# Masked pooling of blocks 3 to 7: transposes and products replaced by running maxima and scans

## The chip, the cores and the metric

The kernel runs on one core of a Trainium2 chip. The metric is device time in microseconds (us) from start to end of one execution. TensorE (PE) does the matrix products, VectorE (DVE), ScalarE (ACT) and GpSimd (POOL) the rest, and SyncE's queue (SP) issues most of the loads. Each engine runs its own instruction list in order; they meet at semaphores.

## The reference

The input is 16 sequences of 256 tokens with 256 features. Four layers follow each other, each added to its input. Layer 0 makes 16 exponential moving averages of a gated input, mixes them and normalises. Layer 1 is the pooling that changes here. Layers 2 and 3 are a mixture of experts and a head, and hold nearly all the products.

```python
attn_in = tanh(hidden @ W1 + b1)
scores  = attn_in @ v                          # one score per token
mask    = where(pt == 0, l <= j, where(pt == 1, l >= j, l != j))
p       = softmax(where(mask, scores[l], -1e30), axis=l)
cnt     = sum(mask, axis=l)
pooled  = einsum('bjl,bld->bjd', p, hidden) / cnt
```

The type `pt` belongs to a sequence. Token j averages over the tokens up to itself (type 0), from itself on (type 1), or over all but itself (type 2). The weight of a token l depends on j only through which tokens are allowed and through the maximum that is subtracted.

## The kernel before

Features lie on the 128 partitions (two halves, h), tokens along the free dimension. A block `b` is two sequences, so 512 tokens; there are 8 blocks. The two sequences of a block are its lanes `s` = 0 and 1, and layers 0 and 1 of one lane of one block (a *unit* below) are cut into 47 pieces `j` = 0 to 46.

**Experts.** The rest of the work is 640 steps. A step takes one block and one chunk of 128 hidden features of one of 9 experts (8 and a shared one) or of the head. Every product there is exact to fp32 by three products of rounded parts (`exact_sum`, L601): each operand is a high part plus a low part. A step of an expert is 18 matmuls of 512 columns: `front(i)` does 6 for the gate and 6 for the up projection, `back(i-3)` does 6 for the down projection of the step three earlier. Per step ACT applies Silu (L1128) and rounds the hidden values (L1159), DVE multiplies gate and up (L1474), and POOL makes the low part (L1620). A new chunk of weights is rounded on ACT (L1089) and its low part taken on DVE (L1439). `front(i)` on PE waits for the DVE product of step i-2. Where a block ends an expert, DVE adds `ps_out` to the sum in `acc` (L1497), and PE's next `back` waits for that.

**Order.** `order()` (L111) writes one list for all engines. After each step it may emit pieces of the units that are due: each piece has a price in `side_cost` (L92), and a step gives a credit of `pace * step_budget`. A lane gets a second piece in the same step only if that piece has no work on PE. `pace` is set so that a block's units are done before the block joins the experts. Semaphores count stages by name (`SIDE_PE`, `SIDE_ACT`, `SIDE_DVE`, `SIDE_POOL`, L279 to L292).

**Pooling before**, pieces 37 to 46 of a unit. PE makes the attention projection (L797) and the score (L626, one column of weights broadcast, so that every partition holds the score row). The mask is a 128 x 512 table of 0 and -1e30 fetched by an indirect DMA that POOL issues at piece 24 (L1597). DVE adds score and mask (L1244), takes the maximum (L1248) and negates it; ACT takes the exponential with its sum (L942). PE transposes the residual (`xT`, L631), ACT and DVE split it in high and low (L946, L1254); DVE scales the probabilities (L1257, L1259, L1262); PE transposes them (L640), they are split too (L949, L1424), and PE multiplies with twelve matmuls of 256 columns (L805). DVE adds the residual (L1431), which ends the unit ("res").

## Time and profile before

| | |
|---|---|
| three runs | 2800.72, 2802.97, 2803.34 us; median 2802.97 |
| profiled execution | 2801.3 us; its span 2799.5 us |
| granted TensorE clock over the span | 0.999 of full |
| busy, share of the span | PE 99%, DVE 64%, ACT 52%, POOL 44% |
| matmuls | 12802 |

An engine's busy time is the time in which it had at least one instruction running. Matmuls overlap: one of 512 columns is shown as 0.39 us long, while the next starts 0.227 us after it. So for PE the distance between starts tells the cost, not the length. "Idle before" is the time in which an engine had nothing running before an instruction, put down to what released it. Shapes are partitions x elements. The names are those of the program, without buffer numbers.

### The profile page before, as it was taken

The page shows a single profiled execution, that of the slowest core. Times are in us where ns is not written, and L with a number is a line of the kernel's source. Part 1 is how long each engine was busy: PE and PEld are TensorE (multiplying, and loading weights), DVE is VectorE, ACT ScalarE, POOL GpSimd, SP SyncE. Part 2 cuts the span into 40 slices and gives each one's busy share as a digit, 9 for nine tenths or more (in the row PEclk, how much of TensorE's full clock was granted, in tenths as well). Part 3 has the DMA queues.
Part 4 walks back from the last instruction along what each step waited for, and adds up shares of the span by engine and source line. Part 5 has one row for each costly group of instructions (what it writes and reads, how often), then busy time and mean ns, then how long its engine had stood idle before and what let it go on. Part 6 is the DMA issues. An engine that isn't in the chain of part 4 may idle for free.

```text
span 2799.5 us, 36722 instructions
## 1 busy us (share of the span) xinstructions
PE 2767.4 (99%) x12802; PEld 2297.9 (82%) x12802; DVE 1798.8 (64%) x2977; ACT 1452.8 (52%) x2634; POOL 1218.7 (44%) x953
## 2 busy tenths in 40 slices
PE   8899999999999999999999999999999999999999
PEld 5678888888878888888888888888888888888888
DVE  8799778867777666557755766555766563333443
ACT  4655656565447544555545644444644563333445
POOL 6266335533554355424543345433454333333334
PEclk9999999999999999999999999999999999999999
DMA  4344333433223322122321332212322131111222
GB/s 152 103 138 126 93 113 110 134 95 108 76 65 107 95 68 68 55 60 72 100 66 58 85 91 74 63 53 57 108 80 64 43 101 46 46 45 46 79 89 58
DMA packets 117383, 230.37 MB, mean 82 GB/s; under 512 B 13672, under 2 KB 58960, under 8 KB 117200
## 3 DMA queue, kind: packets, MB, share of 16 engines
q1 hardware_dynamic: 81808, 190.15, 22.3%
q10 hardware_dynamic: 32832, 29.49, 4.4%
q0 software_dynamic: 2560, 8.39, 1.0%
q8 instruction: 102, 1.67, 0.2%
q14 instruction: 81, 0.66, 0.1%
HBM read 219.89 MB, written 8.09 MB: 81 GB/s over the span
## 4 chain that ended last, share of the span: by engine, by line
PE 95%; DVE 3%; ACT 1%; issue 1%; DMA 0%; POOL 0%; SPq 0%; DVEq 0%; ACTq 0%
PE bank L605 20%; PE bank L606 20%; PE bank L607 20%; PE ps_out L605 10%; PE ps_out L607 10%; PE ps_out L606 10%; PE bank L598 1%; PE ps_out L598 1%; DVE w_lo L1439 1%; DVE trace L1231 0%; DVE hid L1474 0%; DVE trace L1388 0%; PE bank L824 0%; DMA acc<-in_sidew 0%; PE bank L640 0%
## 5 line engine op out<-in xcount | busy, mean ns | idle before, releaser
L1620 POOL TENSOR_TENSOR hid_lo<-hid,hid_hi 128x512 fp32r<-128x512 f32 x640 | 850.2, 1329 | 1527.8 <-ACT hid_hi L1159 1527.5
L605 PE MATMUL bank<-res_lo,w_hi 128*128 128x512 f32 x2428 | 956.2, 394 | 4.7 <-DVE hid L1474 3.8
L606 PE MATMUL bank<-res_hi,w_lo 128*128 128x512 f32 x2428 | 947.3, 390 | 0.0
L607 PE MATMUL bank<-res_hi,w_hi 128*128 128x512 f32 x2428 | 946.3, 390 | 0.0
L1474 DVE TENSOR_TENSOR hid<-hid,bank 128x512 f32<-128x512 f32 x576 | 394.3, 685 | 618.4 <-PE bank L607 590.9
L1128 ACT ACTIVATE hid<-bank 128x512 f32<-128x512 f32 x576 | 343.9, 597 | 587.6 <-PE bank L607 584.7
L1439 DVE TENSOR_TENSOR w_lo<-w_raw,w_hi 128x768 fp32r<-128x768 f32 (+2 forms) x520 | 497.4, 958 | 191.0 <-ACT w_hi L1089 149.0
L1089 ACT ACTIVATE w_hi<-w_raw 128x768 fp32r<-128x768 f32 x392 | 331.3, 845 | 480.6 <-PE ps_out L607 468.6
L605 PEld LDWEIGHTS bank<-res_lo,w_hi 128*128 128x128 f32 x2428 | 456.4, 188 | 97.0 <-DVE w_lo L1439 4.3
L607 PEld LDWEIGHTS bank<-res_hi,w_hi 128*128 128x128 f32 x2428 | 456.1, 188 | 96.6
L606 PEld LDWEIGHTS bank<-res_hi,w_lo 128*128 128x128 f32 x2428 | 456.5, 188 | 89.4
L605 PE MATMUL ps_out<-hid_lo,w_hi 128*128 128x512 f32 (+1 forms) x1344 | 510.1, 380 | 4.5 <-DVE acc L1497 4.5
L607 PE MATMUL ps_out<-hid_hi,w_hi 128*128 128x512 f32 (+1 forms) x1344 | 510.3, 380 | 0.0
L606 PE MATMUL ps_out<-hid_hi,w_lo 128*128 128x512 f32 (+1 forms) x1344 | 509.9, 379 | 0.0
L1159 ACT ACTIVATE hid_hi<-hid 128x512 fp32r<-128x512 f32 x640 | 399.4, 624 | 13.6 <-DVE hid L1474 12.9
L1607 POOL TENSOR_TENSOR temporal<-temporal,trace 128x512 f32<-128x512 f32 x239 | 326.9, 1368 | 22.4 <-DVE trace L1231 22.1
L1231 DVE TENSOR_TENSOR_SCAN trace<-bank,trace 128x256 f32<-128x256 f32 x480 | 304.8, 677 | 8.2
L605 PEld LDWEIGHTS ps_out<-hid_lo,w_hi 128*128 128x128 f32 x1344 | 252.6, 188 | 56.2 <-issue 5.7
L606 PEld LDWEIGHTS ps_out<-hid_hi,w_lo 128*128 128x128 f32 x1344 | 252.7, 188 | 49.4
L607 PEld LDWEIGHTS ps_out<-hid_hi,w_hi 128*128 128x128 f32 x1344 | 252.6, 188 | 47.4
L1388 DVE SCALAR_TENSOR_TENSOR trace<-gated,bl,bank 128x256 f32<-128x256 f32 x448 | 193.4, 473 | 2.0 <-ACT bank L1080 2.0
L1497 DVE SCALAR_TENSOR_TENSOR acc<-ps_out,coef,acc 128x256 f32<-128x256 f32 x288 | 119.4, 476 | 1.9 <-PE ps_out L607 1.5
(223 smaller groups left out, 1604.5 us busy)
## 6 DMA issues: line engine op xcount, KB each, us to landing
w_raw<-in_chunks SPq DMA_DIRECT2D x392, 384.0 KB, 3.1
mod_on<-mod_rows ACTq DMA_DIRECT2D x154, 128.0 KB, 3.2
w_raw<-in_head_chunks SPq DMA_DIRECT2D x64, 224.0 KB, 2.5
stat<-mod_rows ACTq DMA_DIRECT2D x70, 128.0 KB, 3.2
x_in<-in_xT SPq DMA_DIRECT2D x16, 256.0 KB, 3.6
pre_x<-in_xT SPq DMA_DIRECT2D x14, 256.0 KB, 7.1
soma_rows<-pre_soma SPq DMA_DIRECT2D x14, 256.0 KB, 2.0
soma<-soma_rows SPq DMA_DIRECT2D x14, 256.0 KB, 3.7
```

The costliest lines, as they stand in the source:

```text
L605: mm(out, wh, xl, start=start and i == 0, stop=False, skip_group_check=not lone)
L606: mm(out, wl, xh, start=False, stop=False, skip_group_check=not lone)
L607: last = mm(out, wh, xh, start=False, stop=end, skip_group_check=not lone)
L1089: last = activate(w_hi[k][:], raw[:], ACT.Copy)
L1128: activate(h[:], ps_gate[i % 2][:], ACT.Silu).then_inc(s_act, 1)
L1159: activate(hid_hi[i % DEPTH][:], hid[i % 3][:], ACT.Copy).then_inc(s_hhi, 1)
L1231: return V.tensor_tensor_scan(out, decay.broadcast_to([P, S]), x, 0.0, ALU.mult, ALU.add)
L1388: last = STT(tr[:, h, :], gated[s][:, h, :], bl[:, h, d:d + 1], ps[:, 0:S], ALU.mult, ALU.mult)
L1439: return TT(w_lo[k][:, cols], src, f(w_hi[k][:, cols]), ALU.subtract)
L1474: TT(h[:], h[:], ps_up[i % 2][:], ALU.mult).then_inc(s_hid, 1)
L1607: nc.gpsimd.tensor_tensor(temporal[s][:], temporal[s][:], trace[s][d % 3][:], ALU.add).then_inc(l_pool[s], 1)
L1620: nc.gpsimd.tensor_tensor(hid_lo[i % DEPTH][:], hid[i % 3][:], f(hid_hi[i % DEPTH][:]), ALU.subtract).then_inc(s_hlo, 1)
```

## The change

Blocks 0 to 2 keep the pooling above. For blocks 3 to 7 (ten units) `scanned(b)` is true, and pieces 37 to 46 do other work. The score row s is scanned forwards and backwards for a running maximum (`tops`). With m the running maximum, the weighted sum of the tokens up to j obeys sum(j) = exp(m(j-1) - m(j)) * sum(j-1) + exp(s(j) - m(j)) * x(j): a scan with a decay, and the same backwards. Forward sum, own token and backward sum are each weighted by a share, and a share is zero (its exponent -1e30) where the type does not allow that part. The score matrix of 128 x 512, the fetched mask, both transposes, their splits and the twelve matmuls are gone in these units.

```diff
+SCAN_FROM = 3
+def scanned(b):
+    return b >= SCAN_FROM
@@ side_cost
+    if scanned(b) and j > 36:
+        return (0.7, 1.6, 2.3, 1.5, 2.0, 1.4, 1.9, 2.5, 0.4, 2.5)[j - 37]
@@ order
-                    if lane in touched and (j in ON_PE or j == 25):
+                    if lane in touched and (j in ON_PE or j == 25 or scanned(x) and j > 36):
@@ PE: attention projection at 37, score at 38, then nothing more
-                elif j == 38:
+                elif j == (37 if scanned(b) else 38):
+                elif scanned(b):
+                    if j == 38:
+                        score_and_turns(b, s, j)
@@ ACT
+                    elif j == 40:
+                        act.wait_ge(l_dve[s], dve_at(s, b, "grown"))
+                        activate(trace[s][1][:], trace[s][1][:], ACT.Exp).then_inc(l_act[s], 1)
+                        act.wait_ge(l_pool[s], pool_at(s, b, "decay"))
+                        activate(trace[s][2][:], trace[s][2][:], ACT.Exp).then_inc(l_act[s], 1)
+                    elif j == 41:
+                        act.wait_ge(l_dve[s], dve_at(s, b, "shares"))
+                        activate(shares[s][:, 0, 1:S], shares[s][:, 0, 1:S], ACT.Exp)
+                        activate(shares[s][:, 1, 0:S - 1], shares[s][:, 1, 0:S - 1], ACT.Exp)
+                        activate(owns[s][:, 0, :], owns[s][:, 0, :], ACT.Exp).then_inc(l_act[s], 1)
@@ DVE: new pool_by_scans(b, s, j)
+                if j == 38:
+                    V.tensor_tensor_scan(tops[:, 0, :], ones, score, NEG, ALU.mult, ALU.max)
+                    back_scan(tops[:, 1, :], ones, score, NEG, ALU.mult, ALU.max).then_inc(l_dve[s], 1)
+                elif j == 39:
+                    TS(peak, score, no_own, None, ALU.add)
+                    TT(grown[:], score.unsqueeze(1).broadcast_to([P, 2, S]), tops[:], ALU.subtract)
+                    STT(peak[:, later], tops[:, 0, past], no_past, peak[:, later], ALU.add, ALU.max)
+                    STT(peak[:, past], tops[:, 1, later], no_next, peak[:, past], ALU.add, ALU.max)
+                elif j == 40:
+                    STT(shares[s][:, 0, later], ...); STT(shares[s][:, 1, past], ...); STT(own, ...)
+                elif j == 41:
+                    dve.wait_ge(l_act[s], act_at(s, b, "decay"))
+                    V.tensor_tensor_scan(ends[:, 0, :], decay[:, 0, :], grown[:, 0, :], 0.0, ALU.mult, ALU.add)
+                    back_scan(ends[:, 1, :], ...); V.tensor_tensor_scan(steps, ...)
+                elif j == 42:
+                    dve.wait_ge(l_pool[s], pool_at(s, b, "before"))
+                    for h in range(DH):
+                        last = V.tensor_tensor_scan(gated[s][:, h, :], decay[:, 0, :], gated[s][:, h, :], ...)
+                elif j == 43:
+                    dve.wait_ge(l_pool[s], pool_at(s, b, "after"))
+                    ... two backward scans; wait for POOL's "den"; STT(den, steps, more, den, ALU.add, ALU.mult)
+                elif j == 44:
+                    V.reciprocal(den, den); TT(shares 0 * den); TT(shares 1 * den)
+                elif j == 46:
+                    dve.wait_ge(l_pool[s], pool_at(s, b, "parts"))
+                    ... STT(out, own, 1.0, x1) x2; TT(out += gated); TT(out += ema).then_inc  ("res")
@@ POOL: new weigh(b, s, j); the indirect DMA of piece 24 is not issued
+                if j == 39:
+                    ... two MEMSETs of one column; TT(decay 0); TT(decay 1)
+                elif j == 41:
+                    for out, way, name in ((gated[s], 0, "before"), (ema[s], 1, "after")):
+                        TT(out[:], temporal[s][:], grown[:, way, :].unsqueeze(1).broadcast_to([P, DH, S]), ALU.mult)
+                elif j == 42:
+                    G.tensor_copy(den[:, 0:1], own[:, 0:1]); TT(ends 0); TT(ends 1); TT(den); TT(den)
+                elif j == 45:
+                    TT(own, own, den, ALU.mult); TT(gated * share); TT(ema * share)
@@ setup on POOL: 7 operations on 16 columns (kinds, typ); on DVE one MEMSET (unit)
```

Some lines are drawn together here. The new tiles `shares`, `owns` and `dens` lie where `one_hi`, `one_lo` and `two_hi` lie, `ends` is `soma`, and the next block's first pieces wait for "res" of a scanned block instead of "pooled".

What moves on the engines is shown at block 4, lane 0. First DVE, where that unit ends; before (L1431 ends the unit, L1231 is the first scan of the next block):

```order
L1474 TENSOR_TENSOR hid<-hid,bank 128x512 [waits up,activated]
L1424 TENSOR_TENSOR two_lo<-bank,two_hi 128x512 [waits lane0_act]
L1403 TENSOR_TENSOR two_lo<-trace_0,two_hi 128x512 [waits lane1_act]
L1474 TENSOR_TENSOR hid<-hid,bank 128x512 [waits up,activated]
L1431 TENSOR_TENSOR acc<-bank,temporal 128x2x256 [waits y_out0,lane0_pe]
L1231 SCALAR_TENSOR_TENSOR ema<-alpha,x_in_1 128x256 [waits x_in0_1]
L1231 SCALAR_TENSOR_TENSOR ema<-alpha,x_in_1 128x256
L1474 TENSOR_TENSOR hid<-hid,bank 128x512 [waits up,activated]
```

And now (L1594 is the product of the experts, L1374 to L1379 end lane 0's unit, L1333 to L1339 are piece 39 of lane 1, L1559 is the low part of the weights):

```order
L1594 TENSOR_TENSOR hid<-hid,bank 128x512 [waits up,activated]
L1374 SCALAR_TENSOR_TENSOR acc<-owns_53,temporal 128x256 [waits y_out0,lane0_pool]
L1374 SCALAR_TENSOR_TENSOR acc<-owns_53,temporal 128x256
L1377 TENSOR_TENSOR acc<-acc,gated 128x2x255 [waits lane0_dve]
L1379 TENSOR_TENSOR acc<-acc,ema 128x2x255 [waits lane0_dve]
L1333 TENSOR_SCALAR owns_54<-bank,ge 128x256 [waits setup_pool]
L1335 TENSOR_TENSOR trace_1<-bank,trace_0 128x512 [waits lane1_dve]
L1337 SCALAR_TENSOR_TENSOR owns_54<-trace_0,ge,owns_54 128x255 [waits lane1_dve]
L1339 SCALAR_TENSOR_TENSOR owns_54<-trace_0,ge,owns_54 128x255 [waits lane1_dve]
L1559 TENSOR_TENSOR w_lo<-w_raw,w_hi 128x768 [waits w_hi]
L1594 TENSOR_TENSOR hid<-hid,bank 128x512 [waits up,activated]
```

Between two products of the experts DVE now has eight instructions of the two units and the weights, where the stretch shown of before has at most three.

The exponentials on ACT, same unit; before:

```order
L1159 ACTIVATE hid_hi<-hid 128x512
L942 ACT_TABLE_LOAD
L942 ACTIVATE trace_1,den<-trace_0,top 128x256 x2
L946 ACTIVATE one_hi<-bank 128x512
L1128 ACT_TABLE_LOAD
L1128 ACTIVATE hid<-bank 128x512
```

And now (L1174 is the Silu of the experts, L1205 the rounding, L1135 the weights, L1082 the other lane's):

```order
L1097 ACT_TABLE_LOAD
L1097 ACTIVATE trace_1<-trace_1 128x512
L1099 ACTIVATE trace_2<-trace_2 128x512
L1082 ACTIVATE two_hi<-trace_0 128x512
L1174 ACT_TABLE_LOAD
L1174 ACTIVATE hid<-bank 128x512
L1205 ACTIVATE hid_hi<-hid 128x512
L1135 ACTIVATE w_hi<-w_raw 128x768
L1102 ACT_TABLE_LOAD
L1102 ACTIVATE shares_51<-shares_51 128x255
L1103 ACTIVATE shares_51<-shares_51 128x255
L1104 ACTIVATE owns_53<-owns_53 128x256
```

The exponentials come in two pieces, with a table load ahead of each and one behind each.

## Rows read from the trace of the kernel before

**Rows 1.** The page, busy time, share and count of each engine:
```profile
PE 2767.4 (99%) x12802; PEld 2297.9 (82%) x12802; DVE 1798.8 (64%) x2977; ACT 1452.8 (52%) x2634; POOL 1218.7 (44%) x953
```

**Rows 2.** The page, the chain that ended last, shares by engine:
```profile
PE 95%; DVE 3%; ACT 1%; issue 1%; DMA 0%; POOL 0%; SPq 0%; DVEq 0%; ACTq 0%
```

**Rows 3.** Waits of PE: us in total, times, longest:
```profile
PE ps_out L605 <- DVE acc L1497: 4.5, 3, 2.0
PE bank L605 <- DVE hid L1474: 3.8, 5, 1.5
```

**Rows 4.** Timeline of PE: start, us, engine, line, operation:
```profile
2255.57 0.39 PE L605 MATMUL bank<-res_lo,w_hi 128*128 128x512 f32 x1
...
2256.25 0.39 PE L605 MATMUL ps_out<-hid_lo,w_hi 128*128 128x512 f32 x1
...
2264.88 0.60 PE L631 MATMUL bank<-idn,temporal 128*128 128x128 f32 x4
...
2266.71 0.40 PE L605 MATMUL ps_out<-hid_lo,w_hi 128*128 128x512 f32 x1
...
2288.53 0.28 PE L605 MATMUL bank<-two_lo,one_hi 128*128 128x256 f32 x1
...
2289.97 0.40 PE L605 MATMUL bank<-res_lo,w_hi 128*128 128x512 f32 x1
```

**Rows 5.** Groups of PE instructions, shapes apart: count, busy, mean ns, idle:
```profile
L607 PE MATMUL bank<-two_hi,one_hi 128*128 128x256 f32 x56 | 15.9, 284 | 0.0
...
L631 PE MATMUL bank<-idn,temporal 128*128 128x128 f32 x64 | 9.7, 274 | 0.8 <-DVE trace L1244 0.8
```

**Rows 6.** The same of DVE:
```profile
L1439 DVE TENSOR_TENSOR w_lo<-w_raw,w_hi 128x768 fp32r<-128x768 f32 x392 | 436.5, 1116 | 149.2 <-ACT w_hi L1089 149.0
L1474 DVE TENSOR_TENSOR hid<-hid,bank 128x512 f32<-128x512 f32 x576 | 394.3, 685 | 618.4 <-PE bank L607 590.9 <-ACT hid L1128 27.3
L1231 DVE TENSOR_TENSOR_SCAN trace<-bank,trace 128x256 f32<-128x256 f32 x480 | 304.8, 677 | 8.2
L1388 DVE SCALAR_TENSOR_TENSOR trace<-gated,bl,bank 128x256 f32<-128x256 f32 x448 | 193.4, 473 | 2.0 <-ACT bank L1080 2.0
...
L1409 DVE RECIPROCAL stat<-stat 128x256 f32<-128x256 f32 x14 | 24.5, 1752 | 33.2 <-ACT stat L1058 33.2
...
L1244 DVE TENSOR_TENSOR trace<-trace,bank 128x512 f32<-128x512 f32 x16 | 10.9, 683 | 9.5 <-PE bank L626 9.5
...
L1262 DVE TENSOR_SCALAR trace<-trace,den 128x256 f32<-128x256 f32 x32 | 9.9, 351 | 0.6
...
L1431 DVE TENSOR_TENSOR acc<-bank,temporal 128x512 f32<-128x512 f32 x14 | 9.7, 691 | 19.4 <-PE bank L607 19.4
...
L1257 DVE TENSOR_TENSOR den<-den,cnt 128x2 f32<-128x2 f32 x16 | 3.4, 213 | 0.2 <-ACT trace L942 0.2
```

**Rows 7.** DVE line 1375: count: shortest/median/longest ns, first and last start:
```profile
L1375 DVE TENSOR_TENSOR two_lo<-ema,two_hi x14: 679/1191/1765, 122.1 to 1971.6; 128x512 fp32r<-128x512 f32 x14
```

**Rows 8.** The same of DVE line 1254:
```profile
L1254 DVE TENSOR_TENSOR one_lo<-bank,one_hi x14: 683/692/693, 322.3 to 2269.8; 128x512 fp32r<-128x512 f32 x14
```

**Rows 9.** Groups of POOL instructions:
```profile
L1620 POOL TENSOR_TENSOR hid_lo<-hid,hid_hi 128x512 fp32r<-128x512 f32 x640 | 850.2, 1329 | 1527.8 <-ACT hid_hi L1159 1527.5
...
L1597 POOL DMA_INDIRECT trace<-in_penalties,pen_row x16 | 19.8, 1236 | 4.1 <-POOL temporal L1607 2.3 <-issue 0.9
```

**Rows 10.** Group of the table loads ahead of the exponentials on ACT:
```profile
L942 ACT ACT_TABLE_LOAD x14 | 18.0, 1283 | 0.2
```

**Rows 11.** Timeline of ACT behind one unit's exponentials:
```profile
2269.76 1.28 ACT L1126 ACT_TABLE_LOAD   x1
2271.06 0.69 ACT L1126 ACTIVATE hid<-bank,v 128x512 f32<-128x512 f32 x1
```

**Rows 12.** Timeline of PE right after, with its idle time in brackets:
```profile
2271.89 0.47 PE L605 MATMUL bank<-res_lo,w_hi 128*128 128x512 f32 x1 [0.92 <-ACT hid L1126]
...
2275.45 0.47 PE L605 MATMUL ps_out<-hid_lo,w_hi 128*128 128x512 f32 x1 [1.96 <-DVE acc L1497]
```

More of the change, by code:

```diff
@@ L1419, in side @@
                     TT(x1[:], cen[:], X[:], ALU.add).then_inc(l_dve[s], 1)
+                elif scanned(b):
+                    pool_by_scans(b, s, j)
                 elif j in (39, 40, 42):
@@ L1508, in _ @@
             V.memset(eps[:], 1e-5)
+            V.memset(unit[:], 1.0)
             V.memset(stat[0][:, 0:P], 1.0 / D).then_inc(su_dve, 1)
```

137 lines of the change are left out of this document (124 added, 13 removed).

## The prediction

> **What bounds the kernel now.** I read the busy times first, then the chain that ended last, then what PE waited for, then PE's timeline around one unit's pooling. PE is busy 99% of the span [rows 1] and is 95% of the chain [rows 2]. The waits of PE in which something other than a load or the start-up is named come to a few microseconds in the whole run, 4.5 on the sums in `acc` and 3.8 on the product of gate and up [rows 3]. So an instruction taken off PE is worth its distance to the next start, and an instruction added elsewhere costs nothing until it makes PE wait. The reader should look at starts in [rows 4], not at lengths: three matmuls of 512 columns start within 2256.25 - 2255.57 = 0.68 us, so 0.227 each, while each is shown as 0.39 long.
>
> **What the change takes off PE.** Per unit: four transposes of the residual, four of the probabilities, twelve matmuls of 256 columns. The counts agree: 64 transposes of one kind are 4 in each of 16 units, 56 of a kind of the twelve are 4 in each of 14 [rows 5].
> - First transposes: from 2264.88 to 2266.71 are four transposes and six expert matmuls, 1.83 us; six alone take 6 x 0.227 = 1.36; so 0.47 [rows 4]. The second four have the same shape; I take 0.47 again.
> - The twelve: 2289.97 - 2288.53 = 1.44 us [rows 4].
> - Sum 2.38 a unit, ten units: 23.8 us. The projection and the score stay.
> By the profiled execution, 2801.3 - 23.8 = 2777.5. That is the time if PE waits exactly as much as now.
>
> **What it adds on DVE.** Per unit 24 instructions: 9 scans at 0.677 = 6.09, a reciprocal 1.75, 11 of 256 columns at 0.473 = 5.20, three of 512 at 0.69 = 2.07; together 15.1 us. It removes five of 512 columns (the first and last of them are L1244 and L1431, 0.68 to 0.69) = 3.4, two at 0.351 = 0.7, three on two columns at 0.213 = 0.6; together 4.8 [rows 6]. Net 10.3 a unit, 103 in all: DVE goes from 1799 to about 1902, 68%. Scans that run a running maximum, and scans backwards, are not in the trace. Below, they cost the 256-column form (0.473), 9 x 0.2 = 1.8 us a unit less; above, the reciprocal (1.75), 9.7 a unit more. I take the forward scan, which is the nearest row.
>
> Does it reach PE? An expert step is 18 matmuls, 4.09 us. DVE's product can start when twelve have run (2.72) and is needed when `front(i+2)` begins (8.17), so it may be late by 8.17 - 2.72 - 0.69 = 4.8 us. The 618 us that DVE idles ahead of its products say the same [rows 6]. The tightest step I find in the new order is like the one shown for block 4: product 0.69, four instructions of 0.95 + 1.38, piece 39 of the other lane 0.47 + 0.69 + 0.95, weights 1.12 = 6.25 us against 4.09. It leaves DVE 2.2 us late, and the steps behind it are lighter. Adding up such steps through the whole order, the product never gets 4.8 us late. The sum into `acc` has less room. When an expert closes, PE's second half of the next `back` comes 7.49 us after its step began, and DVE's four additions end at 2.72 + 0.69 + 4 x 0.473 = 5.30; 2.2 us of room. The order puts a closing step behind a late DVE about three times, late by 2.7 to 2.9: 1 to 2 us in all. I take 2.
>
> **What it adds on POOL.** Four operations of 512 columns at 1.329 = 5.3, seven of 256, three on one column. The 256-column form is not in my rows: it lies between half of 1.329 and all of it; I take 0.8 (near half, with a fixed part), 5.6. Gone is an indirect DMA, 1.24. Net 9.7, 97 in all (88 to 134): 1219 to about 1316 [rows 9]. The queue behind them is L1620, of which PE's `back` wants the result two steps later; POOL idles 1528 us ahead of it [rows 9], and no step gets more than 1.3 + 3.5 = 4.8 us of POOL work. Counted as nothing; if two such steps were adjacent it would be 1 to 2 us. DVE newly waits for POOL in pieces 42, 43 and 46, and behind DVE's wait stand the next product and the weights' low part. The order puts at least one step between the POOL piece and the DVE piece, so POOL's 4.8 has ended within 0.7 us of the DVE piece's turn: nothing. The setup's seven small operations, at the 0.21 of the smallest DVE row 1.5 us at most, stand in front of POOL's first additions; I take 0.
>
> **What it adds on ACT.** Columns of ACTIVATE are nearly even (1536 before, 1792 after). But the exponentials now come in two pieces, and around each stands a table load: the list has 95 loads where it had 76, 19 x 1.283 = 24 us [rows 10]. ACT goes to about 1477, 53%. One load delays a Silu by 1.3 us, against 4.8 of room as above; in a step of the head (12 matmuls or fewer) the room is smaller. The trace has such a place: block 7, lane 1 did its exponentials there, and PE lost 0.92 to ACT and 1.96 to DVE behind it [rows 12]. In the new order that unit's exponentials lie in expert steps, and those of piece 41 of block 3, lane 1 lie in a head step. One such place goes and one comes: 0 on the sum, 1 us added for the second load of each unit. The Trainium skill (ScalarE: Activation LUTs, "What ACT_TABLE_LOAD costs") puts a switch at 1283 ns for the load and about 1380 for a drain. By that, an estimate, ACT would get 51 us more, and the sum would still hold. The trace has the 1283; of the drain it shows nothing, since the next activation starts at 2271.06, 1.30 after the load's start [rows 11].
>
> **Sum.** 2777.5 + 2 (sums in `acc`) + 1 (ACT) = 2780.5. The profiled execution lies 1.7 us below the median of the runs, so the median should be 2782.
>
> **Rivals.**
> 1. *A small toll in every unit.* Each unit hits one closing step or one table load at a bad moment, for 1 us or so more: 2782 + 10 = 2792. For it: DVE has eight instructions between two products at places. Against: by the same adding up DVE is already late by 3.1 us at steps 148 to 153 of before, and PE waited 4.5 us in all [rows 3].
> 2. *The two table switches stop PE in every unit* as at 2270: 0.92 + 1.96 = 2.9 us in ten units less the one that before paid, 26 us: 2808, which is about where it was, or slower. It decides if exponentials fall in head steps; by the order one of twenty does.
> 3. *DVE and POOL slow each other* (the slower side). A subtraction of 512 columns with both inputs in SBUF takes 0.68 to 1.77 us, median 1.19 [rows 7]; the same with one input in PSUM always 0.69 [rows 8]. Some 17 of the 24 new DVE instructions read SBUF twice, and POOL is given 97 us more to run beside them. At 1.72 times, the heavy step is 0.95 + 1.38 + 0.95 = 3.3 us -> 5.6 of it, 8.6 in all, 4.5 over its step. It decides when DVE enters such a step 0.3 us late or more and closes an expert behind it. If two steps of each unit stop PE by 2 us, that is 40: 2822. Against: the 1.12 of the weights is already the slowed mean, and POOL is idle more than half of the time, also after the change. The Trainium skill (GPSIMD Engine Reference, "Specifications") says that POOL's SBUF interfaces are shared with DVE and contend when DVE has two SBUF inputs. [rows 7] and [rows 8] agree.
> 4. *Waits that before had go as well.* The 2.9 of [rows 12] without a new one in its place, and the ten indirect DMAs no longer beside DVE: 2776.
>
> **How the numbers follow.** Forecast 0.60, rival 1 0.18, rival 2 0.08, rival 3 0.07, rival 4 0.07. The time is the forecast's, 2782; its own range is 2778 to 2787. The range of 8 in 10 takes in rival 4 and rival 1 with some of the way to rival 2: 2773 to 2800. What can be told from no change is 0.2%, 5.6 us. Faster: forecast, rivals 1 and 4, less 0.02 for a toll twice as large: 0.83. Rival 2 is split between same and slower: same 0.08, slower 0.09.
>
> **What would show it.** In the profile of the changed kernel PE has 200 records fewer (12602), and its busy time is about 2744. DVE is near 1902; a value near 1970 speaks for rival 3, and then lines like the shares and the last additions stand above 0.6 us for 256 columns. POOL is near 1316, ACT near 1477 with 24 table loads ahead of exponentials where there are 14. In PE's waits the sums in `acc` and the product stay under 12 us together; near 30 would be rival 2 (with ACT's `hid` named) or 3 (with DVE's). The indirect DMA of the mask appears 6 times. I am wrong about the scans if their backward form is far from 0.68 us; wrong about PE's gain if PE's busy time falls by less than 20.

## The result and the profile after

The changed kernel takes 2812.31 us (median of 7 runs, 2810.20 to 2814.11), the kernel before 2803.04 in the same comparison (7 runs, 2800.72 to 2803.52). The ratio is 1.0031, interval 1.0021 to 1.0041: slower by 0.31%, where 2782 was forecast and 2800 was the upper end of the range. The profiled execution took 2812.31 with a span of 2810.2.

The page after, busy times, and behind them the shares of the chain that ended last:

```profile
PE 2755.4 (98%) x12602; PEld 2276.6 (81%) x12602; DVE 1966.9 (70%) x3118; ACT 1477.9 (53%) x2643; POOL 1342.4 (48%) x1090
...
PE 86%; DVE 7%; ACT 3%; issue 2%; DMA 1%; POOL 0%; ACTq 0%; SPq 0%; DVEq 0%
```

Against [rows 1, 2]: PE has the 200 records fewer that were expected, but its busy time fell by 12.0 us where 23.8 were forecast, and its idle time (span less busy) rose from 2799.5 - 2767.4 = 32.1 to 54.8 us. These two are the whole distance to the 2777.5 that stands for PE waiting as before: 11.8 + 22.7 = 34.5, and 2777.5 + 34.5 = 2812.0. DVE stands at 1966.9, near the 1970 that the prediction gave as the sign of rival 3 (1902 was forecast). What PE waited for, us in total, times, longest:

```profile
PE bank L632 <- DVE hid L1594: 11.6, 10, 1.7
PE ps_out L632 <- DVE acc L1617: 9.5, 8, 2.5
...
PE bank L632 <- DVE two_lo L1493: 6.0, 4, 2.1
PE bank L625 <- DVE one_lo L1524: 3.3, 3, 1.7
```

The first two lines answer to [rows 3], where they were 3.8 and 4.5: 21.1 us together, past the 12 that the forecast allowed. The last two are waits of the *next* block's projections for operands that DVE splits; the prediction's adding up had not followed them at all.

**DVE's new instructions** (groups of the changed kernel, shapes apart: busy, mean ns, idle before):

```profile
L1559 DVE TENSOR_TENSOR w_lo<-w_raw,w_hi 128x768 fp32r<-128x768 f32 x392 | 457.2, 1168 | 129.3 <-ACT w_hi L1135 129.0
...
L1354 DVE TENSOR_TENSOR_SCAN gated<-trace,gated 128x256 f32<-128x256 f32 x20 | 19.3, 1005 | 0.0
...
L1374 DVE SCALAR_TENSOR_TENSOR acc<-owns,temporal 128x256 f32<-128x256 f32 x20 | 17.3, 904 | 3.0 <-POOL ema L1775 2.9
L1347 DVE TENSOR_TENSOR_SCAN soma<-trace,trace 128x256 f32<-128x256 f32 x10 | 17.3, 1727 | 0.0
...
L1325 DVE TENSOR_TENSOR_SCAN soma<-trace,trace 128x256 f32<-128x256 f32 x10 | 12.9, 1293 | 0.0
L1349 DVE TENSOR_TENSOR_SCAN dens<-unit,typ 128x256 f32<-128x256 f32 x10 | 11.8, 1184 | 0.0
...
L1329 DVE TENSOR_TENSOR_SCAN trace<-unit,bank 128x256 f32<-128x256 f32 x10 | 6.8, 684 | 8.3 <-PE bank L653 8.3
...
L1325 DVE TENSOR_TENSOR_SCAN trace<-unit,bank 128x256 f32<-128x256 f32 x10 | 6.6, 660 | 0.0
```

Read two pairs. L1329 is a forward running maximum and the last row a backward one: 684 and 660 ns, so neither direction nor maximum is far from the 677 of [rows 6]. L1347 is the scan of [rows 6] (a product and a sum) on the same 256 columns with its data in SBUF instead of a PSUM bank, and has 1727 ns. The 24 new instructions sum to 20.0 us a unit where 15.1 were forecast, 49 over ten units; the weights' low part, untouched by the change, took 20.7 us more (457.2 against 436.5 [rows 6]).

What stands beside a slow scan shows in the timeline of DVE and POOL in block 4 (start, us), and what PE did a little later:

```profile
1229.41 2.02 DVE L1559 TENSOR_TENSOR w_lo<-w_raw,w_hi 128x768 fp32r<-128x768 f32 x1
1230.57 2.02 POOL L1759 TENSOR_TENSOR gated<-temporal,trace 128x512 f32<-128x512 f32 x1
...
1232.54 1.73 POOL L1759 TENSOR_TENSOR ema<-temporal,trace 128x512 f32<-128x512 f32 x1
1233.05 1.77 DVE L1347 TENSOR_TENSOR_SCAN soma<-trace,trace 128x256 f32<-128x256 f32 x1
1234.75 0.66 DVE L1325 TENSOR_TENSOR_SCAN soma<-trace,trace 128x256 f32<-128x256 f32 x1
...
1238.42 0.68 DVE L1493 TENSOR_TENSOR two_lo<-ema,two_hi 128x512 fp32r<-128x512 f32 x1
...
1239.15 0.39 PE L632 MATMUL bank<-one_lo,side_hi 128*128 128x256 f32 x1 [1.68 <-DVE two_lo L1493]
```

The forward scan lies beside a product of POOL and takes 1.77; the backward one starts 0.48 us after that product ended (1234.27) and takes 0.66. DVE is late with everything behind, and PE stands 1.68 us for an operand that is last in DVE's row.

The long durations are a wait inside the instruction, not a slower pace. The forward scan ends 0.55 us after POOL's product has ended. In the trace of the changed kernel 70 of the new scans read SBUF alone. 31 of them take 0.66 to 0.68 us, and none of these starts while an instruction of POOL has more than 0.12 us left to run. Each of the other 39 (1.00 to 1.81 us) ends 0.545 to 0.552 us after some instruction of POOL ends. The two engines take turns here, and POOL waits too: its product at 1232.54 began under a subtraction of DVE and has 1.73, where the shortest of its kind has 1.29. The kernel before holds the same: each of the subtractions of [rows 7] that takes longer than 0.7 us ends 0.545 to 0.551 us after an instruction of POOL.

**The clock.** In windows of PE alone (us, PE busy and count, granted clock, DMA share, GB/s) the profiled execution of the changed kernel has stretches that the one of the kernel before has not:

```profile
868.00:871.00 3.00, 3.00 (x9) 0.51 0.29 76
902.00:906.00 4.00, 4.00 (x16) 0.57 0.44 153
```

In three such stretches, at 868, 902 and 912, of about 3.4 us each (0.57 over 4 us is 3.4 us at one half), the granted clock is at its lower level (1.2 of 2.4 GHz). Ahead of each PE had stood: 1.91 us before 866.88, 2.53 before 901.56, 2.08 before 912.48. What it costs can be read from starts:

```profile
901.56 0.47 PE L632 MATMUL ps_out<-hid_lo,w_hi 128*128 128x512 f32 x1 [2.53 <-DVE acc L1617]
...
903.72 0.63 PE L632 MATMUL bank<-res_lo,w_hi 128*128 128x512 f32 x1
904.14 0.63 PE L633 MATMUL bank<-res_hi,w_lo 128*128 128x512 f32 x1
904.57 0.63 PE L634 MATMUL bank<-res_hi,w_hi 128*128 128x512 f32 x1
```

0.425 from start to start, where [rows 4] have 0.227. So 3.4 us at the lower level lose 3.4 x (1 - 0.227 / 0.425) = 1.6 us, and three such stretches 4.8 of the 11.8 us that PE's busy time is above the forecast: time that the page books as work. Most of the rest can be estimated from the waits. A wait adds some 0.24 us of busy time: the matmul ahead of it shows its full 0.39 instead of 0.227, and the first one behind it keeps the next for 0.30 (901.56 to 901.86 in the trace). The waits of PE number 47 where they were 26, so this is about 5 us.

The waits alone do not decide whether the clock falls. In e8 below PE stands as long at the same work, and the clock stays at its upper level:

```profile
893.64 0.47 PE L632 MATMUL ps_out<-hid_lo,w_hi 128*128 128x512 f32 x1 [2.55 <-DVE acc L1617]
```
```profile
892.00:899.00 7.00, 5.36 (x29) 1.00 0.54 161
```

And e12 below has a fall in a stretch whose work is that of the kernel before, behind a wait of 1.87 us (before: 1.91, and no fall). The row has the length, then PE, PEld, DVE, ACT and POOL, and the clock of 0.82:

```profile
842.00:847.00 5.00, 5.00 (x20) 4.04 (x19) 3.63 (x7) 1.96 (x3) 2.05 (x1) 0.82 0.45 149
```

The executions of one kernel differ by it too: e5's ten are 2805.1 to 2807.2 us at a mean clock of 0.999 (six) and 2810.4 to 2811.3 at 0.996 or 0.997 (four).

**Where along the kernel.** From each trace I took when each of the 640 steps begins on PE, less the same of before (us; positive is later). The start-up shifts whole runs by up to 4 us, so only differences along a row count, and each row is one execution:

```
first step of the stretch    152    200    304    456    632
after                        0.7   14.5   13.8   14.3   10.7
```

The loss falls in steps 152 to 200, 13.8 us. They hold the two units of block 3, whose pieces stand among the head and closing steps of block 1's experts; most of it comes between steps 178 and 182 (from 3.4 to 15.0 us), in the second unit. Blocks 4 to 7 give back only 3.8, where eight units at 2.38 should give 19.0. That stretch lies at 771 to 980 us of before. Busy time from 780 to 980 (length, then PE, PEld, DVE, ACT and POOL, clock, DMA share, GB/s), before and then after:

```profile
780.00:980.00 200.00, 197.60 (x959) 166.41 (x959) 136.71 (x233) 117.02 (x217) 88.79 (x65) 1.00 0.29 87
```
```profile
780.00:980.00 200.00, 186.09 (x848) 153.04 (x847) 157.39 (x232) 115.06 (x202) 98.35 (x83) 0.97 0.26 80
```

DVE is at 79% there, with as many instructions as before (232 and 233) and 20.7 us more of work.

### The profile page after: what moved, and what is told of

It is laid out like the page before. It is cut to its first block, busy times and chain, and to the rows that moved or that the text cites. A ratio compares the mean times of both kernels' runs of the same rounds, so it can differ in the third digit from the quotient of the medians.

```text
span 2810.2 us, 36617 instructions
## 1 busy us (share of the span) xinstructions
PE 2755.4 (98%) x12602; PEld 2276.6 (81%) x12602; DVE 1966.9 (70%) x3118; ACT 1477.9 (53%) x2643; POOL 1342.4 (48%) x1090
## 4 chain that ended last, share of the span: by engine, by line
PE 86%; DVE 7%; ACT 3%; issue 2%; DMA 1%; POOL 0%; ACTq 0%; SPq 0%; DVEq 0%
PE bank L632 18%; PE bank L633 18%; PE bank L634 18%; PE ps_out L632 9%; PE ps_out L634 9%; PE ps_out L633 9%; DVE w_lo L1559 2%; PE bank L625 1%; PE ps_out L625 1%; DVE hid L1594 1%; DVE trace L1277 1%; DMA w_raw<-in_chunks 0%; ACT w_hi L1135 0%; ACT L1174 0%; DVE trace L1506 0%
## 5 line engine op out<-in xcount | busy, mean ns | idle before, releaser
L1789 POOL TENSOR_TENSOR hid_lo<-hid,hid_hi 128x512 fp32r<-128x512 f32 x640 | 862.8, 1349 | 1412.6 <-ACT hid_hi L1205 1412.1
L1594 DVE TENSOR_TENSOR hid<-hid,bank 128x512 f32<-128x512 f32 x576 | 393.5, 683 | 522.9 <-PE bank L634 498.8
L1174 ACT ACTIVATE hid<-bank 128x512 f32<-128x512 f32 x576 | 343.8, 597 | 581.8 <-PE bank L634 578.7
L1559 DVE TENSOR_TENSOR w_lo<-w_raw,w_hi 128x768 fp32r<-128x768 f32 (+2 forms) x520 | 517.5, 997 | 164.4 <-ACT w_hi L1135 129.0
L1135 ACT ACTIVATE w_hi<-w_raw 128x768 fp32r<-128x768 f32 x392 | 331.1, 845 | 462.7 <-PE ps_out L634 442.5
L1205 ACT ACTIVATE hid_hi<-hid 128x512 fp32r<-128x512 f32 x640 | 398.9, 623 | 32.4 <-DVE hid L1594 31.3
L1738 POOL TENSOR_TENSOR temporal<-temporal,trace 128x512 f32<-128x512 f32 x239 | 329.2, 1378 | 20.2 <-DVE trace L1277 19.4
```

The source lines that it names most:

```text
L1135: last = activate(w_hi[k][:], raw[:], ACT.Copy)
L1174: activate(h[:], ps_gate[i % 2][:], ACT.Silu).then_inc(s_act, 1)
L1205: activate(hid_hi[i % DEPTH][:], hid[i % 3][:], ACT.Copy).then_inc(s_hhi, 1)
L1559: return TT(w_lo[k][:, cols], src, f(w_hi[k][:, cols]), ALU.subtract)
L1594: TT(h[:], h[:], ps_up[i % 2][:], ALU.mult).then_inc(s_hid, 1)
L1738: nc.gpsimd.tensor_tensor(temporal[s][:], temporal[s][:], trace[s][d % 3][:], ALU.add).then_inc(l_pool[s], 1)
```

## Experiments

Theory A: DVE and POOL hold each other up, and DVE's lateness reaches PE (rival 3). Theory B: the table switches on ACT do it (rival 2). Theory C: the new order or prices. Theory D: plainly more work on DVE, whoever works beside it. Each run is given by its distance to the kernel before in its own comparison (the changed kernel: +9.3 us); half an interval is about 3 us, in e8 4.8 and in e11 and e14 to e16 3.4 to 3.9. All but e3 are the changed kernel with the edits named. Differences in the text are taken before rounding. The last two columns are how many us later (or, negative, earlier) the profiled execution gets against before over steps 152 to 200 and over 200 to 632. In e12 the first of them is 1.6 though its work there is that of before, by one fall of the clock; so differences of 2 us in these columns say little.

```
                            median   ratio [interval]          to before  152-200  200-632
changed kernel              2812.31  1.0031 [1.0021, 1.0041]    +9.3      +13.8     -3.8
e1 POOL pieces shortened    2797.20  0.9976 [0.9966, 0.9985]    -6.2       +9.1    -14.2
e2 no exponentials          2802.07  0.9993 [0.9983, 1.0003]    -1.4       +9.6    -10.9
e8 both                     2783.34  0.9934 [0.9917, 0.9951]   -21.4       +1.0    -20.2
e3 before, new prices       2802.49  0.9992 [0.9983, 1.0002]    -0.9       -0.1     -0.3
e9 reciprocal shortened     2809.30  1.0019 [1.0009, 1.0029]    +4.6      +11.4     -5.7
e5 decays in PSUM           2806.95  1.0014 [1.0005, 1.0024]    +3.5       +9.8     -6.3
e6 e5, one table visit      2808.07  1.0014 [1.0004, 1.0023]    +3.4       +7.7     -5.0
e7 e6 from block 4          2801.77  0.9994 [0.9985, 1.0004]    -3.0        0.0     -2.2
e4 from block 4             2802.35  0.9997 [0.9988, 1.0007]    -2.2        0.0     -1.5
e12 e5 from block 4         2803.24  0.9992 [0.9983, 1.0002]    -1.3       +1.6     +1.5
e10 two products on DVE     2806.28  1.0009 [0.9999, 1.0018]    +1.8      +10.7     -6.8
e11 e12, four on DVE        2793.92  0.9972 [0.9960, 0.9984]   -10.6        0.0     -8.9
e13 e5, four on DVE         2798.52  0.9984 [0.9975, 0.9993]    -4.6       +6.6    -12.6
e14 e13, no exponentials    2785.09  0.9938 [0.9924, 0.9952]   -18.1       +1.1    -19.7
e15 e11, one table visit    2793.86  0.9964 [0.9951, 0.9978]    -9.3        0.0    -11.0
e16 e13, one table visit    2793.34  0.9964 [0.9951, 0.9978]    -9.9       +3.7    -13.5
```

### Taking each suspect away

**e1_pool_short** leaves most columns out of POOL's five products of pieces 41 and 45 (so the pooled values are not the reference's):

```diff
-                        TT(out[:], temporal[s][:], grown[:, way, :].unsqueeze(1).broadcast_to([P, DH, S]),
-                           ALU.mult).then_inc(l_pool[s], 1)
+                        TT(out[:, 0, 0:1], temporal[s][:, 0, 0:1], grown[:, way, 0:1], ALU.mult).then_inc(l_pool[s], 1)
```

> The changed kernel, but POOL's operations of pieces 41 and 45 (two of 512 columns, one of 256 and two of 510 in each of the ten units, about 6.7 us a unit in its profile) work on one column each; DVE, ACT and PE do the same as in the changed kernel (the values of the pooled part are then not the reference's). Changed kernel 2812, before 2803. Theory port (DVE instructions with two inputs in SBUF are slowed where POOL runs beside them, and PE then waits for DVE): the slowed new DVE lines (scan of soma 1.73 us, scan of gated 1.00, additions into acc 0.90) fall towards 0.66 and 0.47, DVE's busy time falls from 1967 by 25 to 40 us, and the time to about 2795. Theory load (DVE has too much to do even at undisturbed durations): DVE's busy time hardly moves and the time stays at 2808 to 2813. Theory tables: 2812.

Measured: 15.5 us less than the changed kernel. DVE, whose instructions are all there, fell from 1966.9 to 1934.2. Its rows of L1325 and L1349:

```profile
L1349 DVE TENSOR_TENSOR_SCAN dens<-unit,typ 128x256 f32<-128x256 f32 x10 | 6.6, 660 | 0.0
L1325 DVE TENSOR_TENSOR_SCAN soma<-trace,trace 128x256 f32<-128x256 f32 x10 | 6.6, 660 | 0.0
```

1184 and 1293 ns became 660, with nothing changed but what POOL does beside them. That is theory A's mechanism by itself. L1347 only fell to 1286: beside it often stands POOL's rounding product of the experts, which was there before. The edit also shortens what DVE waits for from POOL (2.9 us ahead of L1374 became 0.6), so not all of the 15.5 need be turns lost to POOL.

**e2_no_switch** replaces each of the five exponentials by a copy of a constant 1 (the weights are wrong):

```diff
-                        activate(trace[s][1][:], trace[s][1][:], ACT.Exp).then_inc(l_act[s], 1)
+                        activate(trace[s][1][:], trace[s][1][:], ACT.Copy, bias=1.0, scale=0.0).then_inc(l_act[s], 1)
```

> The changed kernel with its five exponentials per scanned unit replaced by copies that write 1.0 (no activation table is switched for them: 56 table loads in the list instead of 95; pooled values are then not the reference's). Theory tables (the two switches per unit hold up Silu and the rounding, and through them DVE and PE): the time falls by 10 us or more, to 2802 or below. Theories port and load: by 0 to 4 us, 2808 to 2812, because ACT is 53% busy.

Measured: 10.6 us less. DVE's products wait 10.0 us for ACT's Silu instead of 23.4. Theory B is a part too, and rival 2's mechanism can be seen in block 3, in a step of the head (ACT and PE of the changed kernel; start, us; idle in brackets):

```profile
892.08 1.28 ACT L1172 ACT_TABLE_LOAD   x1
...
893.38 0.69 ACT L1172 ACTIVATE hid<-bank,v 128x512 f32<-128x512 f32 x1
...
894.21 0.47 PE L632 MATMUL bank<-res_lo,w_hi 128*128 128x512 f32 x1 [0.86 <-ACT hid L1172]
```

Further on DVE's additions into `acc` end late and PE has the 2.53 us of idle time shown above.

**e8_both** makes both edits.

> The changed kernel with both cuts at once: POOL's operations of pieces 41 and 45 on one column each, and the exponentials as copies of 1.0 without a table switch (values not the reference's). Matmuls and the list of DVE's operations are those of the changed kernel. If port and tables are separate and add up: 2812 - 15 - 10 = 2787. If what remains above 2779.5 (before less the removed products) is DVE's plain load, it is 5 to 10 us. If one stop is paid by either: 2793 to 2797.

Measured: 30.7 us less than the changed kernel, where the two alone give 26.1; 2783.34, within 1.4 us of the forecast of 2782. Its page:

```profile
PE 2746.0 (99%) x12602; PEld 2274.2 (82%) x12602; DVE 1925.0 (69%) x3118; ACT 1427.4 (51%) x2604; POOL 1285.1 (46%) x1090
```

PE is busy 2746.0, 21.4 us less than before; 2744 was forecast. In 780 to 980 its clock is back at 1.00. So the work taken off PE is worth about what the prediction said, and the two suspects together account for the miss, the clock's part included. That the two together give 4.5 us more than their sum is within the uncertainty of this run (four executions).

**e3_order_only** is the kernel *before* with only the new prices and the one-step rule for those pieces.

```diff
+    if b >= 3 and j > 36:
+        return (0.7, 1.6, 2.3, 1.5, 2.0, 1.4, 1.9, 2.5, 0.4, 2.5)[j - 37]
```

> The kernel before, all pooling as before, but with the new prices of pieces 37 to 46 of blocks 3 to 7 and the new rule that these pieces take one step per lane. Theory order (the new prices move the pieces of blocks 1 to 7 to worse places, whatever they contain): 2810 or more. Theories port, load and tables: within 3 us of before, 2800 to 2806.

Measured: no difference from before. Theory C falls, as far as the order goes without the new instructions in it.

**e9_recip_short** takes the reciprocal on one column (the ten took 17.4 us of DVE; the divisor is wrong):

```diff
-                    V.reciprocal(den, den).then_inc(l_dve[s], 1)
+                    V.reciprocal(den[:, 0:1], den[:, 0:1]).then_inc(l_dve[s], 1)
```

> The changed kernel, but the new reciprocal of DVE (128x256, 1.74 us, once per unit, one input, not slowed beside POOL) works on one column: 16 us of plain DVE time less, nothing else (values not the reference's). Theory load: the time falls by a good part of that, 6 to 12 us, to 2800 to 2806. Theory port: 0 to 4 us, since piece 44 carries no wait of PE and POOL's work stays.

Measured: 4.7 us less, with intervals that overlap. If it is taken as it stands, DVE's own work has a price near 0.3 us for each us here, where the forecast had it at nothing. But four of the ten executions have a mean clock of 0.999 or more (2806.2 to 2807.1 us) and six have 0.996 or 0.997 (2809.0 to 2812.1), so the clock can be a part of the 4.7; the run doesn't part the two.

### Keeping the results, moving the collision

**e5_decay_psum** has ACT write the decays into a free PSUM bank, and so the six scans read one operand from there:

```diff
-                        activate(trace[s][2][:], trace[s][2][:], ACT.Exp).then_inc(l_act[s], 1)
+                        act.wait_ge(l_dve[s], dve_at(s, b, "shares"))
+                        activate(both, trace[s][2][:], ACT.Exp).then_inc(l_act[s], 1)
```

> The changed kernel, same results, but the decays are written by ACT into the lane's PSUM bank instead of into trace 2, so that the six scans with a decay per unit read one input from SBUF and one from PSUM; ACT waits for piece 40 of DVE before it writes. Number and length of all operations stay. Theory port: these scans all take 0.66 to 0.68 us (now 1.73, 1.29, 1.00 twice, 0.88 twice, so 3.7 us a unit less than their 6.8), DVE's busy time falls by about 28 us, the time by 5 to 15 to about 2802. Theory load: the six scans are as slow as now or the time stays at 2812 although they are faster. Theory tables: 2812 or a little more, because ACT waits once more.

Measured: 5.8 us less; DVE 1939.2. The scan's row, and the decay scans of the state:

```profile
L1355 DVE TENSOR_TENSOR_SCAN gated<-bank,gated 128x256 f32<-128x256 f32 x20 | 12.6, 670 | 0.0
...
L1348 DVE TENSOR_TENSOR_SCAN soma<-bank,trace 128x256 f32<-128x256 f32 x10 | 6.8, 680 | 0.0
```

1005 became 670 and 1727 became 680, with POOL's work where it was. A scan with one operand in PSUM takes no turns with POOL: L1348 has its 0.68 us with POOL's products still running beside it. But 28 us of DVE's busy time bought only 5.8 of the kernel's. (ACT now also waits for piece 40 of DVE before it writes.)

**e6_one_switch** (e5 with all five exponentials in piece 40: one visit to their table a unit, 75 loads) and **e7_one_switch_from4** (the same with `SCAN_FROM = 4`):

```diff
-                    elif j == 41:
-                        act.wait_ge(l_dve[s], dve_at(s, b, "shares"))
```

> The version with the decays in PSUM (2807), same results, and all five exponentials of a unit in piece 40, behind DVE's shares: 75 table loads in the list instead of 95. Measured so far against the changed kernel's 2812: port (POOL cut short) -15, tables (no switch) -10, decays in PSUM -5. Theory port and tables, both real and adding up: about half of the tables' 10 us on top of the 5, so 2800 to 2803, within 0.2% of before. Theory that the PSUM version already took what the switches cost (one shared stop): 2806 to 2808.

> The same version, but scans from block 4 on, so that block 3, whose pieces 41 to 46 fall among the short head steps of block 1 (176 to 183), pools as before. In the changed kernel PE lost 13.8 us against before between steps 152 and 200, where that unit lies, and only gained in the rest. Theory place (most of the loss is that block's collision with the head steps): faster than e6 by 5 to 10 us, 2792 to 2797, and no dip of the granted clock behind the start-up. Theory toll (every unit loses about the same, so fewer units give less loss and less gain): within 3 us of e6.

Measured: e6 is no better than e5 (+3.4, +3.5). e7 is 6.3 better than e6, and cannot be told from before.

**e4_from4** (the changed kernel with `SCAN_FROM = 4`) and **e12_psum_from4** (e5 with it):

> The changed kernel with the scans from block 4 on (8 units instead of 10), same results. By the lag of the steps against before, the changed kernel loses 13.8 us between steps 152 and 200, where block 3's second unit stands among the closing steps of block 1, and gets 3.8 us back over blocks 4 to 7. If the place of block 3 is what costs, the loss of 13.8 us goes and the time is 2799 +-3 us. If every unit pays alike (+9.3 us over 10 units), it is 2810 +-3 us. If the ported load is only shifted one block on, a like loss of some 10 us shows in block 4 and the time is 2808 to 2812.

> Scans from block 4 on and decays in PSUM, the multiplies left on GpSimd and the exponentials in two pieces; same results. Beside the version with one switch a unit (2801.8 us) it tells whether a table switch less a unit is worth anything once it is no longer beside block 3: if the number of switches counts (10 us were seen when all 20 went), this one is 4 us slower, 2806; if only their place in block 3 did, it is 2801 +-2 us.

Measured: e4 lies 11.5 us below the changed kernel, and it gets that in steps 152 to 200. So the place in block 3 is a cost of its own, and no like loss moved to block 4; but the other eight units still earn about 1.5 us instead of 19.0. In e12 PSUM for the decays earned nothing more (-1.3), and its distance to e7 (1.7) is within the uncertainty: beyond block 3 neither edit shows alone.

**e10_wide_on_dve** puts POOL's two products of piece 41 on DVE, ahead of the scans that read them:

```diff
-                    dve.wait_ge(l_pool[s], pool_at(s, b, "before"))
+                    TT(gated[s][:], x1[:], grown[:, 0, :].unsqueeze(1).broadcast_to([P, DH, S]),
+                       ALU.mult).then_inc(l_dve[s], 1)
+                    mine("mul_b")
```

> The changed kernel with GpSimd's two broadcast multiplies of piece 41 (20 of them, 1.67 us each) put on VectorE, ahead of the scans that read them; same results. If VectorE is late because it works beside GpSimd, VectorE's load rises by some 24 us but its scans and 512-column operations fall back towards their lone durations: half of the 15 us that shortening both GpSimd pieces gave, less some 4 us for 24 us more of plain VectorE work (3 us for 16 us was measured): 2808 +-4 us. If it is the sum of VectorE's work that makes it late, whoever works beside it, the kernel gets slower: 2820 +-5 us.

Measured: 7.5 us less, as theory A had it (2808 +-4), and far from D's 2820. Its page shows the exchange:

```profile
PE 2754.1 (98%) x12602; PEld 2274.6 (81%) x12602; DVE 1968.6 (70%) x3138; ACT 1478.1 (53%) x2643; POOL 1306.6 (47%) x1070
...
L1352 DVE TENSOR_TENSOR gated<-temporal,trace 128x512 f32<-128x512 f32 x10 | 10.5, 1047 | 0.0
...
L1359 DVE TENSOR_TENSOR ema<-temporal,trace 128x512 f32<-128x512 f32 x10 | 7.7, 772 | 0.0
```

DVE took over 20 instructions, 18.2 us, and its busy time rose by 1.7. POOL lost 35.8. What DVE gained from not having POOL beside it paid for the work it took over. With DVE's sum equal, the time still fell by 7.5. It was not a wait of DVE for POOL that went: the changed kernel has only one in the pieces of the pooling,

```profile
DVE acc L1374 <- POOL ema L1775: 2.9, 1, 2.9
```

and e10 keeps it (3.1). What got lighter are the steps: piece 41's scans are down to 1286, 660 and 660.

**e11_dve_from4** has all four 512-column products on DVE, the decays in PSUM, from block 4 on; **e13_dve_from3** is the same from block 3 on; **e14_dve_no_switch** is e13 with copies of 1 for the exponentials (the weights are wrong).

```diff
+                elif j == 45:
+                    mine("scaled")
+                    for x, way, at_, to in ((gated[s], 0, past, later), (ema[s], 1, later, past)):
+                        TT(x[:, :, at_], x[:, :, at_], shares[s][:, way, to].unsqueeze(1).broadcast_to([P, DH, S - 1]),
+                           ALU.mult).then_inc(l_dve[s], 1)
```

> Scans from block 4 on, decays written to PSUM by ScalarE, and all four wide multiplies of a unit on VectorE instead of GpSimd; same results. If GpSimd's wide multiplies beside VectorE are the toll of a unit, this is the fastest correct version: 2798 - 8/10 x 3.5 = 2795 +-4 us. If VectorE's own sum decides, it is slower than the version with the multiplies on GpSimd (2801.8 with one table switch): 2808 +-5 us.

> The version with four wide multiplies of a unit on VectorE and the decays in PSUM, from block 3 on (10 units); same results. From block 4 on these multiplies on VectorE were worth 9.3 us (2793.9 against 2803.2) over 8 units. If they are worth the same in a unit of block 3, this one is 2808 - 12 = 2796 +-3 us, and the steps 152 to 200 lose some 7 us against before where 9.8 were lost. If block 3's second unit is held up by GpSimd's share alone, the loss there goes and the time is 2790. If it is the table switches that hold it up, the loss there stays at 8 to 10 us and the time is 2799 to 2803.

> The same kernel with the five exponentials of a unit replaced by copies of a constant 1 (the weights are then wrong, and the table switches are gone); scans, products and transfers stay. Where GpSimd's multiplies were shortened and the switches were gone, the time was 2783 us, and the steps 152 to 200 lost 1 us. If moving the multiplies to VectorE removes the same toll as shortening them, this one is 2783 + 4 (48 us more of plain VectorE work) = 2787 +-4 us, with no loss in steps 152 to 200. If VectorE's own work is the toll that is left, it is 2795 or more.

Measured: e11 is 9.3 us below e12, and beats the kernel before (0.9972, interval 0.9960 to 0.9984). A part of the 9.3 may be the clock: among executions with a mean clock of 0.999 the medians are 2799.6 and 2793.0, 6.6 apart. DVE did 5.6 us more work in it than in e12, POOL 42.8 less:

```profile
PE 2751.9 (99%) x12642; PEld 2277.8 (82%) x12642; DVE 1918.0 (69%) x3122; ACT 1472.2 (53%) x2642; POOL 1269.7 (45%) x1032
```

e13 lies 8.1 below e5, with 6.6 us still lost in steps 152 to 200: between the expectations, so that place is held by more than one cause. e14 shows the other: with the table visits gone too the loss there is 1.1, blocks 4 to 7 give back 19.7 (19.0 was due), and PE's waits are near those of [rows 3]:

```profile
PE ps_out L632 <- DVE acc L1628: 6.8, 7, 1.9
...
PE bank L632 <- DVE hid L1605: 3.9, 4, 1.5
```

The 20 visits are worth 13.4 us in e13, 5.5 of them in block 3's stretch.

**e15_dve_one_switch4** and **e16_dve_one_switch3** are e11 and e13 with one visit a unit (edit as in e6):

> Wide multiplies on VectorE, decays in PSUM, scans from block 4 on, and the five exponentials of a unit in one piece of the list, so with one visit to their table in place of two; same results. Taking all 20 visits away was worth 13.4 us in the version from block 3 on. If each visit costs alike, 8 fewer are worth 5 us: 2789 +-3 us. If a unit's second visit costs little beside the first (or the longer single piece on ScalarE delays its Silu as much as two switches do), it stays at 2794 +-2 us.

> The same from block 3 on; same results. If each visit to the table costs alike, 10 fewer are worth 6.7 us: 2792 +-3 us. If the toll is set by the place where a visit stands in block 3's second unit, among closing steps, and one visit is still there: 2797 to 2799 us, with 4 to 6 us still lost in steps 152 to 200.

Measured: e15 equals e11. e16 is 5.2 us below e13 by the medians, with intervals that overlap; the two profiled executions are equal (2795.25 and 2795.04), and e16's gets 2.9 us less late in steps 152 to 200. From block 4 on the second visit of a unit costs nothing that can be told; beside block 1's closing steps it seems to. So the place of a visit seems to count more than the number, which these runs suggest and don't show. e16, which leaves nothing out, is the changed kernel's idea at 0.9964 of before (0.9951 to 0.9978). e11, e15 and e16 can't be told apart.

## Why the prediction was wrong

- **PE's saving, 23.8 us: right within 3 us.** e8 and e14 show PE busy 21.4 and 21.0 us less than before, and blocks 4 to 7 giving back 20.2 and 19.7 for 19.0.
- **DVE's durations: the step that failed.** Nine scans at 0.677 were summed from a row whose first operand is in a PSUM bank [rows 6]; seven of the nine new ones read SBUF alone, and their means go up to 1.73 us. The bounds that I wrote were about the kind of scan, and the kind turned out to cost nothing. What costs is the turn that DVE loses when both its operands are in SBUF and POOL is in the middle of an instruction: up to 1.15 us on a scan of 0.66. The spread was on the page already: 0.68 to 1.77 for a subtraction out of SBUF [rows 7], always 0.69 with PSUM [rows 8]. I cited both under rival 3, as a factor of 1.72 and not as a wait for POOL's instruction to end, and gave it 0.07, on the grounds that the weights' 1.12 was "already the slowed mean" and POOL idle half of the time. Neither held: the weights' mean rose to 1.168 as well, and POOL's pieces of a unit do not lie anywhere in its idle half but beside DVE's pieces of the same unit and of the other lane, as the timeline of block 4 shows. The Trainium skill (GPSIMD Engine Reference, "Specifications") says that POOL shares its SBUF interfaces with DVE and that they contend when DVE has two SBUF inputs; e1 (660 for 1293) and e5 (680 for 1727) agree from both sides. That DVE ended near rival 3's 1970 is partly luck: the new instructions are 49 us above the forecast and the weights' low part 20.7, which rival 3 did not price; other lines are some 5 us lower.
- **"Does it reach PE?": wrong on two counts.** With the lone durations the product was never to be 4.8 us late, and e8 bears that out (PE waits for it 4 times, 3.9 us; before 5 times, 3.8). With 65 us more of DVE work than forecast, PE waited for it ten times where it had been five. And the adding up followed the products and the sums into `acc` only. The operands that DVE splits for the next unit's projections stand last in DVE's row and cost 9.3 us in the last two lines of PE's waits after.
- **Two table visits for 1 us, "one such place goes and one comes": wrong in size.** Taken away they are worth 10.6 to 13.4 us; ACT's own time was right (1477.9 for 1477). In block 3 a visit did fall in a step of the head, at 892, and cost PE 0.86 us directly. The rest seems to go through the product: DVE's waits for the Silu fall from 23.4 to 10.0 us in e2, though the kernel before had 27.3 with more room behind them. A margin of 4.8 us was granted to ACT and to DVE each, while both draw on the same one. Which visits cost how much was not measured one by one.
- **POOL, 1316: 1342 measured.** Seven operations of 256 columns at 0.8 were right (5.7 us a unit for 5.6); the four wide ones are 5.9 for 5.3, the three small ones, put at nothing, 0.74, and the untouched rounding products grew by 12.6 us (850.2 [rows 9] to 862.8). "Counted as nothing" missed that POOL's time is paid on DVE.
- **Rival 3's size** was 2822, by 4 us in each unit. The whole loss, of all causes, was 19.0 - 3.8 = 15.2 in the eight units from block 4 on, 1.9 each, and 13.8 + 4.8 = 18.6 in block 3's two. Of the 30.7 us that e8 takes back, half goes with POOL's pieces alone (15.5) and a third with the table visits alone (10.6); the last 4.5 are within the uncertainty. So rivals 2 and 3 were both partly true.
- **The clock** was in no term. 4.8 us of the miss are PE at the lower level, in three stretches that follow waits of some 2 us.

What stays open: in e8 and e14 the two units of block 3 still lose 1 us where they should save 4.8. The waits that are left there are those of e8 for the sums in `acc`, 1.92 us before 862.1 and 2.55 before 893.6; what makes the sums late was not tried. Nor is it known what makes the clock fall behind one such wait and not behind another: from 780 to 980 it is 1.00 in e8, with both these waits.

## What to carry to other kernels

Price an instruction moved to VectorE by where its operands are and by what GpSimd does at the same moment, not by the mean of its kind. If all its operands are in SBUF, add what is left of the GpSimd instruction that runs when it starts; where a change hands one unit's work to both engines at once, expect that wait often. Putting one operand in PSUM takes the wait away, and giving GpSimd's part to VectorE too costs VectorE little; the second was worth 7 to 9 us here, the first 6 at most. And when several engines are each "hidden by 4.8 us", it is one margin: add up their delays in a step before calling any of them free, and follow every operand that stands last in a row, not just the loudest two.

## What the runs showed of the hardware

- A scan or running maximum of 256 columns takes 0.66 to 0.69 us forwards or backwards (reversed access on input and output), with an operand in PSUM or with POOL idle. With all operands in SBUF it waits for an instruction of POOL that is running, and ends 0.55 us after that one: the ten of L1347 in the changed kernel have

```profile
L1347 DVE TENSOR_TENSOR_SCAN soma<-trace,trace x10: 1181/1782/1805, 841.7 to 2260.1; 128x256 f32<-128x256 f32 x10
```

(shortest, median, longest). A column that is broadcast counts as such an operand too: L1349 reads `unit` and `typ` alone, both one column wide, and took 0.66 to 1.72 us.
- The turns are not shared out evenly. DVE's low part of the weights (128x768) has 0.95 us in most places where it stands alone. When POOL's instructions follow each other without a gap, it does not get between them: at 2289.87 it waited through eight of them (one an indirect DMA) and ended 0.82 us after the last.

```profile
2289.87 9.13 DVE L1559 TENSOR_TENSOR w_lo<-w_raw,w_hi 128x768 fp32r<-128x768 f32 x1 [0.57 <-ACT w_hi L1135]
```

- POOL's instructions hold such waits as well. Its product of 512 columns with a broadcast operand takes 1.29 us alone, as long as the rounding one (median 1.29), and its copy of one column 0.18; a MEMSET of one column takes 0.10. In the changed kernel, beside DVE, they have (shortest, median, longest):

```profile
L1759 POOL TENSOR_TENSOR ema<-temporal,trace x10: 1288/1677/1748, 844.5 to 2262.9; 128x512 f32<-128x512 f32 x10
```
```profile
L1764 POOL COPY dens<-owns x10: 178/581/913, 850.0 to 2269.8; 128x1 f32<-128x1 f32 x10
```

- After waits of 1.9 to 2.5 us PE's granted clock was at its lower level for some 3.4 us, three times within 50 us. After the 1.68 us in block 4 it stayed at the upper one (1.00 from 1236 to 1246), and so it did after 2.55 us in e8 (1.00 from 892 to 899).
